# One product for the value weights of two sequences, copied into place by DMA

## Time and profile before

| | |
|---|---|
| median of 3 runs | 555.71 us |
| the profiled execution | 557.2 us |
| its span, first to last instruction | 555.4 us |
| mean granted TensorE clock | 0.972 of full |
| PE busy | 507.8 us, 91% |
| DVE busy | 438.9 us, 79% |
| ACT busy | 343.8 us, 62% |
| POOL busy | 250.5 us, 45% |

### The profile page before, as it was taken

One profiled execution on the slowest core, in us unless ns is written; L12 is line 12 of the kernel. 1 busy time (PEld: TensorE's weight loads), 2 busy tenths in 40 slices (PEclk: granted clock), 3 DMA queues, 4 the chain that ended last, 5 costly groups with the idle time before them and its releaser, 6 DMA issues.

```text
span 555.4 us, 7269 instructions
## 1 busy us (share of the span) xinstructions
PE 507.8 (91%) x2174; PEld 366.0 (66%) x2174; DVE 438.9 (79%) x794; ACT 343.8 (62%) x608; POOL 250.5 (45%) x217
## 2 busy tenths in 40 slices
PE   6999986978779999899999999999997999979992
PEld 2465552845557687488768867885885788767771
DVE  2899999997799477989967985897677567868783
ACT  3657539786598474667466656765663766557453
POOL 0133050400223256556935664574335156737776
PEclk9999999899898999999999999999997999989997
DMA  8960202210021032000000000002111136255752
GB/s 299 316 194 2 76 1 76 76 44 33 0 77 63 15 77 77 0 2 0 2 1 1 0 0 1 2 1 76 40 38 39 38 128 235 91 159 157 222 153 71
DMA packets 28101, 39.98 MB, mean 72 GB/s; under 512 B 7421, under 2 KB 19838, under 8 KB 27776
## 3 DMA queue, kind: packets, MB, share of 16 engines
q1 hardware_dynamic: 24656, 31.10, 18.0%
q0 software_dynamic: 3408, 8.43, 4.1%
HBM read 25.70 MB, written 16.83 MB: 77 GB/s over the span
## 4 chain that ended last, share of the span: by engine, by line
PE 51%; DVE 6%; issue 6%; POOL 4%; ACT 3%; DMA 1%; SPq 0%; POOLq 0%; ACTq 0%; DVEq 0%
PE psum L1452 35%; PE psum L1542 7%; PE psum L1255 3%; PE psum L1394 2%; PE psum L1513 2%; PE psum L1340 1%; POOL gru L1005 1%; DVE gru L1865 1%; POOL sorted_rows L1035 1%; DVE slots_full L1867 1%; POOL out L1043 1%; POOL slots_lo L1020 1%; PE psum L1352 1%; DVE gru L1845 1%; PE psum L1416 1%
## 5 line engine op out<-in xcount | busy, mean ns | idle before, releaser
L1452 PE MATMUL psum<-slots_hi,w_hh 128*128 128x512 f32 x560 | 181.5, 406 | 1.2 <-ACT gru L752 1.2
L1452 PEld LDWEIGHTS psum<-slots_hi,w_hh 128*128 128x128 f32 x560 | 104.5, 191 | 27.8 <-issue 4.2
L1005 POOL TENSOR_TENSOR gru<-slots_full,gru 128x512 f32<-128x512 f32 x43 | 65.7, 1529 | 111.8 <-ACT gru L758 111.8
L1452 PE MATMUL psum<-slots_lo,w_hh 128*128 128x512 f32 x280 | 112.0, 400 | 0.0
L1452 PE MATMUL psum<-at,v_ih_pair 128*128 128x512 f32 x288 | 91.4, 402 | 5.0 <-DVE at L1744 3.1
L758 ACT ACTIVATE gru<-gru,vec 128x512 f32<-128x512 f32 x48 | 34.7, 722 | 58.7 <-DVE gru L1845 58.6
L1452 PEld LDWEIGHTS psum<-at,v_ih_pair 128*128 128x128 f32 x288 | 53.7, 190 | 21.9 <-DVE at L1744 3.4
L1838 DVE SCALAR_TENSOR_TENSOR gru<-psum,vec,gru 128x512 f32<-128x512 f32 x48 | 35.9, 747 | 36.0 <-PE psum L1452 30.2
L1138 PE MATMUL psum<-early_hi,w_in 128*128 128x512 f32 x128 | 57.9, 611 | 5.3 <-DMA early_hi<-in_xT 5.2
L1452 PEld LDWEIGHTS psum<-slots_lo,w_hh 128*128 128x128 f32 x280 | 53.4, 191 | 12.9
L1865 DVE TENSOR_TENSOR gru<-gru 128x512 f32<-128x512 f32 x47 | 43.7, 929 | 7.2 <-POOL gru L1005 3.7
(11 more groups left out here) (249 smaller groups left out, 878.3 us busy)
## 6 DMA issues: line engine op xcount, KB each, us to landing
gathered<-sorted_rows SPq DMA_DIRECT2D x39, 129.0 KB, 2.5
x_scratch<-slots_full SPq DMA_DIRECT2D x8, 512.0 KB, 3.0
x_block<-x_scratch SPq DMA_DIRECT2D x8, 512.0 KB, 4.1
early_hi<-in_xT SPq DMA_DIRECT2D x3, 1024.0 KB, 5.4
x_tm<-in_x SPq DMA_DIRECT2D x4, 512.0 KB, 6.3
slots_full<-expert_plus SPq DMA_DIRECT2D x1, 2048.0 KB, 10.3
sorted_rows<-gru SPq DMA_DIRECT2D x1, 1032.0 KB, 11.7
early_hi<-in_xT SPq DMA_DIRECT2D x2, 512.0 KB, 4.6
```

The costliest lines, as they stand in the source:

```text
L1005: pool.tensor_tensor(DF(u), full[:, c, seq(k, h), blk(j)], X(u), ALU.subtract).then_inc(d_pool, 1)
L1452: last = pe.matmul(psum[:, bank, :], w, d, start=start and i == 0, stop=stop and i == len(pairs) - 1, skip_group_check=begun or late)
```

## The change

One product now serves two sequences. The stationary operand holds the 64 value columns of two sequences side by side, so that a matmul's 128 rows are sequence 0 of the pair on partitions 0 to 63 and sequence 1 on 64 to 127. There are four steps `i` (pair, half of the columns) where there were eight. ACT copies the high and low parts to one of three buffers (`value_parts`, 128 by 384 numbers), and SP sends each filled buffer on with four transfers (`spread_value`): two sequences, each to both halves of the partitions of `v_ih`. Parts are numbered 0 to 7 (high 0, high 1, low 0, low 1 of the first pair, then of the second) and part n uses buffer n mod 3; ACT waits for the transfers that last read a buffer before it fills it again. The first GRU unit of each pair waits for all of the pair's transfers.

The first pair's steps stand where steps 0 and 1 stood. The second pair's stand after `transposes(1)`.

```diff
+        vp_out = [sem(f"vp_out_{i}") for i in range(3)]
...
+        value_parts = [sb2(f"value_part{i}", [P, G3 // 2], F32R) for i in range(3)]
...
-        v_sb = gru[:, 3:5, :].rearrange("p c (b h m) -> p c b h m", b=B, h=2)
+        v_sb = gru[:, 3:5, 0:B * M].rearrange("p c (b m) -> p c b m", b=B)
...
         def value_bank(i):
-            return TBS[i % 2] if i < B else VB + i % 2
+            return TBS[i % 2] if i < 2 else VB + i % 2
+
+        def high_part(i):
+            return 4 * (i // 2) + i % 2
...
+                def spread_value(w, pair):
+
+                    for n in range(4 * pair + 2 * w, 4 * pair + 2 * w + 2):
+                        h = n % 2
+                        sp.wait_ge((vp_hi, vp_lo)[w], 2 * pair + h + 1)
+                        for b in range(2):
+                            for to in range(2):
+                                sp.dma_start(v_ih[pair][half(to), b, w, h * HG:(h + 1) * HG].bitcast(F32),
+                                             value_parts[n % 3][half(b), :].bitcast(F32)).then_inc(vp_out[n % 3], 16)
...
                 load_tm(2)
+                spread_value(0, 0)
+                spread_value(1, 0)
                 load_tm(3)
-                for b in range(B):
+                save(0)
+                spread_value(0, 1)
+                spread_value(1, 1)
+                for b in range(1, B):
                     save(b)
...
-                        twice = psum[:, OB + c, 0:BM].rearrange("p (b h m) -> p b h m", b=B, h=1).broadcast_to(
-                            [P, B, 2, M])
-                        act.activation(v_sb[:, c], twice, ACT.Copy).then_inc(v_ev, 1)
+                        act.activation(v_sb[:, c].rearrange("p b m -> p (b m)"), psum[:, OB + c, 0:BM],
+                                       ACT.Copy).then_inc(v_ev, 1)
...
+                def free_part(n):
+                    if n > 2:
+                        act.wait_ge(vp_out[n % 3], 64 * (n // 3))
+
                 def value_high(i):
-                    b, h = i // 2, i % 2
                     act.wait_ge(vp_mm, i + 1)
-                    act.activation(vp(0, b)[:, h * HG:(h + 1) * HG], psum[:, value_bank(i), 0:HG],
+                    free_part(high_part(i))
+                    act.activation(value_parts[high_part(i) % 3][:], psum[:, value_bank(i), 0:HG],
                                    ACT.Copy).then_inc(vp_hi, 1)

                 def value_low(i):
-                    b, h = i // 2, i % 2
                     act.wait_ge(vp_sub, i + 1)
-                    act.activation(vp(1, b)[:, h * HG:(h + 1) * HG], psum[:, value_bank(i), 0:HG],
+                    free_part(high_part(i) + 2)
+                    act.activation(value_parts[(high_part(i) + 2) % 3][:], psum[:, value_bank(i), 0:HG],
                                    ACT.Copy).then_inc(vp_lo, 1)
...
@@ ACT's list
                 row_roots(0)
-                value_high(2)
-                value_high(3)
                 values(3, 0)
-                value_low(2)
-                value_low(3)
                 second_rows(0)
...
                 window(3)
-                value_high(4)
-                value_high(5)
+                value_high(2)
+                value_high(3)
                 first_rows(2)
-                value_low(4)
-                value_low(5)
+                value_low(2)
+                value_low(3)
                 new_slots(1)
                 spread_roots(0, OB)
                 low_slots(1)
-                value_high(6)
-                value_high(7)
                 window(4)
-                value_low(6)
-                value_low(7)
                 first_exponentials()
...
@@ PE's list
                 output(1)
-                value_input(2)
-                value_input(3)
-                project(3, 0, 1)
-                value_rest(2)
-                value_rest(3)
-                project(3, 1, C)
+                project(3)
...
                 transposes(1)
-                value_input(4)
-                value_input(5)
-                value_rest(4)
-                value_rest(5)
+                value_input(2)
+                value_input(3)
                 spread(0, OB)
-                value_input(6)
-                value_input(7)
+                value_rest(2)
+                value_rest(3)
                 low_parts(1)
                 first_scores(0, S_B)
-                value_rest(6)
-                value_rest(7)
...
+                    if q == 0 and k < 2:
+                        for i, done in enumerate(vp_out):
+                            pe.wait_ge(done, 64 * len(range(i, 4 * k + 4, 3)))
                     run(r_bank(u), update(0), start=False).then_inc(r_mm, 1)
```

More of the change, by code:

```diff
@@ L1213, in value_input @@
                 def value_input(i):
-                    b, h = i // 2, i % 2
+                    pair, h = i // 2, i % 2
                     if i == 0:
@@ L1281, in first_hidden @@
                     else:
-                        pe.wait_ge(vp_lo, 2 * B - 1 + q)
+                        pe.wait_ge(vp_lo, 3 + q)
                     h, j, c = place(q)
```

14 lines of the change are left out of this document (6 added, 8 removed).

## The result

The changed kernel takes 560.67 us (median of 9 runs, 558.73 to 562.26); the kernel before, timed in turn with it, 557.70 (9 runs, 554.62 to 558.53). The ratio is 1.0054, 95% interval 1.0037 to 1.0071: **3.0 us slower**, where +1.6 was forecast. 560.67 lies above the range given (554.5 to 559.8). Of the miss of 3.4 us, 2.0 are the base, whose median was 555.71 in the three runs that stood ahead of the prediction; 1.4 are the change. On that older base, 1.0054 times 555.71 would be 558.7 us, inside the range.

What follows compares the result with a forecast made beforehand. DVE's list was taken to set the pace until about 128 us, with ACT's list, scores and DVE the path from 115 to 130. Parts 1 to 6 at 0, plus 0.1 and 1.5, gave +1.6: 557.3 us, range 554.5 to 559.8.

Steps and rivals of the forecast that it cites:

- Part 1: At 75 to 90 us, first pair's removed PE and ACT steps: hidden by DVE's full list, 0; uncovered, up to 1.7.
- Part 8: Scores, from 126.11 us: PE, idler ahead of them, falls to 1.2 GHz; costs 1.5 to 2.1 us, 1.5 taken.
- Parts 5 and 6: Transfers of first and second pair: landed at 69.0 and 118.7 us, early enough for ACT's buffer reuse; 0 each.
- Parts 2, 3, 4 and 7: Stationary copy, two products at 119.88, copies and subtractions behind: 0 each; first GRU unit's three new semaphore waits: 0.1 us.
- A: The forecast itself: PE's clock falls ahead of the scores; 557.3 us, chance 0.52.
- B: All hidden: PE keeps its clock ahead of the scores; 555.8 us, chance 0.22.
- D: ACT waits for buffer 1 ahead of new_slots(1), delaying scores and DVE; 558.6 to 562.3 us, chance 0.09.
- E: Sixteen issues or buffer waits hold up something costed at nothing (load_tm(3), save); +1 to +2 us, chance 0.03.
- C: Slack from 105 to 130: ACT's freed 1.7 us reaches the scores, at most DVE's 1.31 goes; 554.4 us, chance 0.14.

Runs made afterwards that it cites:

- f1r2: Changed kernel plus three useless matmuls ahead of output(2)'s second half, and the two removed products back ahead of the scores: 557.69 us, ratio to before 0.9998.
- r1_front: Changed kernel with the first pair's removed PE and ACT work put back at its old place, results unused: 559.17 us, ratio to before 1.0025.
- few_transfers: Changed kernel with 16 transfers of 128 partitions in place of 32 of 64, same bytes: 560.28 us, ratio to before 1.0049.
- r12_both: Changed kernel with the first pair's removed work and the second pair's two removed products back, all transfers kept: 556.88 us, ratio to before 0.9985.
- v1_moved: Changed kernel with the second pair's value steps moved ahead of output(2)'s second half, nothing left out: 556.95 us, ratio to before 0.9989.
- v3_full: Changed kernel, second pair's steps moved earlier, plus useless matmuls filling PE's gaps from the row sums to the scores: 555.18 us, ratio to before 0.9970.
- r2_scores: Changed kernel with the second pair's two removed products put back on PE ahead of the low parts, result unused: 558.01 us, ratio to before 1.0009.
- warm_before: Kernel before plus four useless matmuls between the last projection and the transposes of sequence 2: 558.20 us, ratio to before 1.0015.
- v2_fill4: Changed kernel, second pair's steps moved earlier, plus four useless matmuls between row sums and low parts: 557.17 us, ratio to before 0.9991.
- f1_fill: Changed kernel plus three useless matmuls on PE between low parts of sequence 0 and output(2)'s second half: 558.34 us, ratio to before 1.0021.

## Why the prediction was wrong

**Part 1 failed: "Value: 0".** ACT's side of it held: its wait ahead of the roots grew to 4.25 us (at most 4.5 was said), and DVE's timeline from 60 to 105 moved by 0.15 us. But the sentence "DVE does not wait for either in this stretch" took PE's work to last as long as before. I did not ask what being early does to PE itself: it was idle from 102.5 to 106.4, 3.89 us where 0.73 had been, the low level came with the work behind that, and DVE waited 2.9 us more. The forecast's own sign of error, DVE moving by more than 0.5 us between 60 and 128 us, came at 110. The 2.7 us taken off PE's list are not what opened the hole, as they ended in a wait for ACT at 82.0 us. ACT's gates were 1.4 us earlier, and the low stretch of 94.6 to 101.4 no longer held up the work ahead of the hole, 1.7 us. That a low stretch lay so near could be read before. f1r2, where matmuls of no use and no copy of ACT bring the time of before back (0.9998), shows that it was the clock.

**Part 8 was right in place and mechanism, and in size by luck.** The scores were to take over 4.5 us, at a clock below 1.00, with a wait above 2 us: 5.80 us, 0.50, and 2.91. The cost was 1.5 by forecast and is 1.6 by DVE's wait. But the low level lasted from 122.6 to 132.8, 10.2 us, not 3.1 to 4.3, and 4.4 us of it lay in the scores. The loss came to 1.6 as the first loss gave them 0.6 us more of a lead. With the first place repaired it is 2.5 us (3.84 less 1.31, r1_front), which is above the 2.1 that I took as the end of the range.

**The sum** therefore was 1.6 where the two waits make 4.5 and the medians 3.0. That the losses hide 0.6 us of each other is read from the lead of the scores in two profiles; the medians do not show it, as the first repaired alone gives 1.5 us, the second alone 2.7, and both 3.8. An end of the range built from both places (2.9 + 2.5, less what they hide of each other) would have held the result.

**Parts 5 and 6 held.** ACT's second low copy started at 68.97, forecast 69.0. The buffer that value part 4 had filled was free in time; the transfers (96 KB in the profile; the 98 of part 6 are the same bytes in thousands) landed after 2.2 us, where 3.0 was taken, and took 0.60 us to issue, where 0.51 was, two errors that largely cancel. **Parts 2, 3, 4 and 7** show no cost: ACT's list to the scores has the same length, and the unit's first wait is 3.14 us for DVE as before. The Trainium skill's rule against transfers to separate halves (*DMA: Bandwidth & Descriptors*, "Rules for kernel authors"), set against part 6, has no effect here that can be measured: few_transfers saves sixteen of them, and its ratio is 1.0049 to the changed kernel's 1.0054.

**The rivals.** A was the right mechanism with half of its places. B (all hidden) and D (ACT waits for a buffer) are excluded by the rows, E by r12_both and few_transfers. C's idea, that work taken off ACT could bring the scores forward, is right at another place: v1_moved shortens ACT's list ahead of the scores and v3_full then removes DVE's wait of 1.31 us altogether.

**What stays open.** What decides where a low stretch falls. Holes of 3.89 us and, in r2_scores, of 2.65 us brought it, one of 2.81 in warm_before did not, and the same list had it at 105.5 to 112.3 in the changed kernel's execution and shorter, behind 2.70 us of idle time, in that of few_transfers. The runs show that it moves when work ahead of it moves, not by what rule. The Trainium skill (*TensorE: Matmul & The Clock Gate*, "HAM oscillation — how this bites in real kernels") tells of a kernel in which one wait for a transfer per round of work brought the half rate each time. That idle time brings it holds here for v3_full against v2_fill4, though in the latter no gap behind 116 us was longer than 1.48 us; that this gap or that one will, no run lets me say. Nor is it known how often each of these kernels has the low stretches of its one profile. The low stretches behind 160 us lie at slightly other times in each profile, and part of the scatter of the whole times may be theirs.

## What to carry to other kernels

When work is taken off PE, or off an engine that PE waits for, follow the time it frees to the next places where PE waits, and read in the granted clock whether the work behind that gap runs at the low level and who waits for it; busy time alone says "hidden". A low stretch of the kernel before that costs nothing is a warning: edits ahead of it were followed here by low stretches in places that do cost (the change itself, warm_before). Fill such gaps with real work first (v1_moved, 3.7 us), and if the gap lies ahead of a product on the path, fill it wholly: half-filled it bought nothing (v2_fill4), filled it gave 1.8 us by the medians (v3_full, 555.18 against v1_moved's 556.95) and 1.1 by the ratios.

## What the runs showed of the hardware

- Matmuls of no use on PE made one kernel faster (f1_fill, 558.34 us, against the changed kernel's 560.67) and, at another place, another one no faster and by a hair slower (warm_before, ratio 1.0015, 1.0001 to 1.0029).
- The same program is granted the low clock for more or less of its time from one execution to the next: few_transfers ran at a mean clock of 0.957 or 0.958 four times and once at 0.973, 1.4 to 2.3 us faster. One profile is one sample of that.
- The clock also fell where PE had no gap longer than 1.48 us in the 20 us and more ahead (v2_fill4, 0.50 in 124 to 130).
- Transfers of 96 KB within the on-chip memory landed 2.2 us after issue and took SP 0.60 us each to issue, against 3.0 and 0.51 for the 512 KB ones of L441.
